# Embedding tower on one core: one store for the codes of all halves, an earlier load of codes and x tile, and an earlier transpose

## The reference

```python
# e: 2048 x 16 x 16, e[:, t] = tbl_t[ids[:, t]]
A = jnp.repeat(r_x0, 16, axis=1)                           # 2048 x 624 x 16
Bm = jnp.repeat(e, 39, axis=2).reshape(2048, 624, 16)
z = jnp.einsum('bnh,bnd,nk,khd,kd->bkh', A, Bm, alpha, w, hv[..., 0])
h = jnp.concatenate([z.reshape(2048, 256), dense_ctx], axis=1)
h = jnp.maximum(h @ W_top1 + b_top1, 0.0)     # 272 -> 512
h = jnp.maximum(h @ W_top2 + b_top2, 0.0)     # 512 -> 256
y = h @ W_top3                                # 256 -> 1
```

## Time and profile before

| | us |
|---|---|
| median of 3 runs | 180.37 |
| the three runs | 180.37, 179.28, 182.56 |
| the profiled execution's own time | 178.92 |
| its span | 177.0 |
| TensorE busy (matmul) | 164.0, 93% |
| VectorE busy | 142.5, 80% |
| GpSimd busy | 110.9, 63% |
| ScalarE busy | 66.0, 37% |

### The profile page before, as it was taken

The page is one execution under the profiler, slowest core; times in us unless marked ns, Lnnn a source line. Parts: engine busy times, 40 slices in busy tenths (PEclk is TensorE's granted clock), DMA queues, the critical chain, the costliest instruction groups (busy, mean ns, idle before and its releaser), DMA issues.

```text
span 177.0 us, 5041 instructions
## 1 busy us (share of the span) xinstructions
PE 164.0 (93%) x2131; PEld 124.3 (70%) x2131; DVE 142.5 (80%) x177; ACT 66.0 (37%) x176; POOL 110.9 (63%) x116
## 2 busy tenths in 40 slices
PE   6549898968997999999999999999999999999993
PEld 1338696736984879696969696969686967776671
DVE  2978797893799999999899979996999899495000
ACT  3440788084881125212431243123403341451141
POOL 2777777777747777777777777777777776000000
PEclk9999999996999999999999999999999999999999
DMA  5889999999999997989498948694559360000000
GB/s 87 307 120 327 246 275 161 270 373 264 283 334 250 345 320 150 363 248 230 79 352 240 216 160 300 189 230 104 183 219 222 48 231 6 2 4 0 0 4 0
DMA packets 15085, 34.26 MB, mean 194 GB/s; under 512 B 6618, under 2 KB 10582, under 8 KB 11990
## 3 DMA queue, kind: packets, MB, share of 16 engines
q1 hardware_dynamic: 10162, 31.51, 58.9%
q0 software_dynamic: 3584, 0.92, 6.6%
q10 hardware_dynamic: 1316, 1.50, 2.9%
HBM read 33.88 MB, written 0.04 MB: 192 GB/s over the span
## 4 chain that ended last, share of the span: by engine, by line
PE 69%; DMA 13%; DVE 4%; ACT 3%; SPq 3%; issue 3%; POOL 3%; DVEq 0%
PE bank L927 17%; PE bank L842 17%; PE bank L848 15%; PE bank L894 11%; DMA ids_half_dram<-ids_half 6%; PE bank L915 5%; PE bank L835 4%; DMA ids_b<-ids_half_dram 3%; POOL e L478 3%; DMA e<-tbl_dram,ids_all 3%; DVE prod L642 2%; SPq L446 2%; DMA ids_all<-ids_dram 1%; ACT apart L724 1%; PE bank L856 1%
## 5 line engine op out<-in xcount | busy, mean ns | idle before, releaser
L478 POOL DMA_INDIRECT e<-tbl_dram,ids_all x112 | 110.7, 988 | 38.7 <-issue 33.2
L642 DVE TENSOR_TENSOR prod<-x,bank 128x2048 f32<-128x2048 f32 x40 | 90.3, 2279 | 8.8 <-issue 4.6
L927 PE MATMUL bank<-prod,m_w 128*32 128x256 f32 x640 | 38.6, 382 | 2.5 <-DVE prod L642 2.5
L894 PE MATMUL bank<-table,onehot 125*128 125x64 bf16 (+1 forms) x288 | 31.9, 198 | 2.3 <-DVE low L537 2.3
L842 PE MATMUL bank<-tower,w_z 128*128 128x256 f32 x128 | 32.8, 403 | 0.7 <-ACT tower L743 0.7
L894 PE MATMUL bank<-low,onehot 125*128 125x64 bf16 (+1 forms) x288 | 31.8, 197 | 0.0
L894 PE MATMUL bank<-rest,onehot 125*128 125x64 bf16 (+1 forms) x288 | 31.8, 199 | 0.0
L894 PEld LDWEIGHTS bank<-table,onehot 125*128 125x128 bf16 x288 | 27.4, 98 | 5.7 <-issue 2.9
L927 PEld LDWEIGHTS bank<-prod,m_w 128*32 128x32 f32 x640 | 19.1, 109 | 17.0 <-issue 3.5
L848 PE MATMUL bank<-tower,w 128*128 128x256 f32 x128 | 30.7, 382 | 0.1
L842 PEld LDWEIGHTS bank<-tower,w_z 128*128 128x128 f32 x128 | 24.2, 199 | 6.3 <-ACT tower L743 3.1
(11 more groups left out here) (60 smaller groups left out, 85.4 us busy)
## 6 DMA issues: line engine op xcount, KB each, us to landing
x<-x_dram SPq DMA_DIRECT2D x16, 1024.0 KB, 8.1
x<-x_dram SPq DMA_DIRECT2D x16, 512.0 KB, 12.4
ids_b<-ids_half_dram SPq DMA_DIRECT2D x7, 576.0 KB
e<-tbl_dram,ids_all POOLq DMA_INDIRECT x112, 4.7
prod<-windows_c_dram ACTq DMA_DIRECT2D x1, 768.0 KB
prod<-windows_c_dram ACTq DMA_DIRECT2D x1, 512.0 KB, 5.6
w_z<-w_z_dram SPq DMA_DIRECT2D x1, 512.0 KB
w<-w_dram SPq DMA_DIRECT2D x1, 512.0 KB, 11.0
```

The source lines that it names most:

```text
L478: nc.gpsimd.indirect_dma_start(out=e[:, tile, f * D:(f + 1) * D], out_offset=None, in_=t[f"tbl_{f}"][:, :], in_offset=bass.IndirectOffsetO ...
L642: nc.vector.tensor_tensor(prod[:, s % NPROD, :].rearrange("p (q b) -> p q b", q=HP), x0[:, tile % NX, :].rearrange("p (q b) -> p q b", q=H ...
L894: made = nc.tensor.matmul(o_bank[i % 2][:, at:at + m * D], onehot[:, n % 2, g, HOT.index(f), tile * P:(tile + 1) * P], parts[part][:, KT_A ...
L927: made = nc.tensor.matmul(z_bank[q * ZW:(q + 1) * ZW, a * HB:(a + 1) * HB], m_w[:, UNIT_OF[g], hp * ZW:(hp + 1) * ZW], prod[:, s % NPROD, ...
```

## The change

All 72 rows of codes go to DRAM by one DMA at the place where half 1's store stood; the six later stores and SyncE's wait for them are gone. On SyncE the load of half 2's codes moves ahead of `b_w3`, and x tile 3 ahead of `ctx` and `w1_z`; x tile 4 moves ahead of half 3's codes and `w2`. On TensorE turn (0, 2) moves ahead of pick 5.

```diff
-        ids_stored = [sem(f"ids_stored_{n}") for n in range(2)]
+        ids_stored = sem("ids_stored")
...
-            sp.dma_start(ids_rows[1], ids_half[1:IDS:NH, :]).then_inc(ids_stored[0], 16)
+            sp.dma_start(ids_rows.rearrange("n f b -> f n b"), ids_half[:]).then_inc(ids_stored, 16)
...
-            sp.wait_ge(ids_stored[0], 16)
+            sp.wait_ge(ids_stored, 16)
             load_ids(1)
             sp.wait_ge(gathered[0][0], 16 * 2 * len(GATHERED[0][0]))
             load_x0(1)
             load_x0(2)
-            for n in range(2, NH):
-                sp.dma_start(ids_rows[n], ids_half[n:IDS:NH, :]).then_inc(ids_stored[1], 16)
+            load_ids(2)
             sp.dma_start(b_w3[:], t["b_w3"]).then_inc(in_b_w3, 16)
+            load_x0(3)
             load_ctx()
             sp.dma_start(w1_z[:], t["w1_z"].rearrange("(a p) n -> p a n", p=P)).then_inc(in_w1, 16)
-            sp.wait_ge(ids_stored[1], 16 * (NH - 2))
-            load_ids(2)
-            load_x0(3)
+            load_x0(4)
             load_ids(3)
             sp.dma_start(w2[:], t["w2"].rearrange("(a p) n -> p a n", p=P)).then_inc(in_w2, 16)
-            load_x0(4)
...
                 if s == 2:
                     for unit in CONTRACTS[2]:
                         contract(unit)
+                    turn_windows(0, 2)
                     for i in PICKS[2]:
                         pick_rows(i)
...
-                if s == 1 or g == 2:
+                if s == 1 or g == 2 and n > 0:
                     turn_windows(n, g)
```

## The result

The changed kernel takes 184.18 us, median of 4 runs (182.02 to 185.93). The kernel before, run beside it, takes 179.82 (4 runs, 179.02 to 182.56). The ratio is 1.0246, 95% interval 1.0176 to 1.0316: about 2.5% slower, where 1.1% faster was forecast, and outside the range. Runs of one kernel scatter by several us here, and the ratios are made from undisturbed runs alone, so a ratio and its two medians needn't agree.

A forecast was written before the change was run, and what follows sets the result against it. TensorE alone sets the end from about 57 us. Step 5 gains 2.5 us, but half 3's codes hold contract 7 to 53.9 instead of 55.87: 2.0 us, so 180.37 becomes 178.4, range 176.4 to 181.5.

The forecast's parts named there:

- The one store: Codes to DRAM: one 36 KB store for seven of 4.5 KB costs 0, with 0 to 1 us allowed.
- Half 2's codes: SyncE's load behind x tile 2: lands by 33.3 to 34.1 us instead of 36.2, so ScalarE leaves the path.
- The turn: TensorE's turn (0, 2) ahead of pick 5: step 3 starts at 33.04, contract 4 ends at 38.6, gain 0.84 us.
- The mark: Contract 7, TensorE's last contraction that has to wait, at 55.87 us; arriving there sooner shortens the run by the same amount.
- `w1_z` lands at 39.2, 0.6 us of waiting: TensorE behind contract 4: the load lands between 38.1 and 40.3 us, middle 39.2, and is wanted at 38.6.
- The base, 33.9: Landing of `w1_z` in the kernel before: 36.2 less the 2.3 us that half 2's codes need at 255 GB/s.
- A second term: Half 3's codes, with x tile 4 now ahead of them: land between 45.1 and 46.3 us, taken as 45.4.
- the prediction's own 8.5 us: ScalarE's path: contract 7 can't start earlier than 8.5 us after `find_apart(3)`, which gave 53.9 us.
- The clock: Rival, chance 0.22: TensorE's clock falls to 1.2 GHz again, l1 loses 1.65 us, gain 0.9, 179.5 us.
- The loads keep pace: Rival, chance 0.15: `w1_z` at 38.1, half 3's codes before 44.2, contract 7 at 52.8, gain 3.0, 177.4 us.
- Half 3's codes come late: Rival, chance 0.13: they land after 47.4 us, contract 7 passes 55.87, slower, say 182.0 us.
- It doesn't do what it says: Rival, chance 0.08: turn (0, 2) waits for a late gather, or the store delays half 1's codes; 180.4 us.

The follow-up runs named there:

- e9: The changed kernel again, unaltered: 183.00 us, ratio 1.0179 to the kernel before.
- e8: The kernel before with the single store for seven, every load in its old order: 180.09 us, ratio 0.9923.
- e15: The changed kernel with `ctx_x` split, the columns of halves 0 and 1 at the old place, the others behind x tile 9: 178.22 us, ratio 0.9936.
- e4: The changed kernel with fourteen products of zeros on TensorE ahead of the wait for `w1_z`: 181.46 us, ratio 1.0157.
- e1: The changed kernel with x tile 3 back behind `w1_z`: 182.84 us, no ratio.
- e6: The changed kernel with x tile 4 back behind `w2`, tile 3 still ahead of `w1_z`: 180.62 us, ratio 0.9984.
- e3: The changed kernel with `w1_z` ahead of the four `ctx` loads: 181.32 us, ratio 1.0007.
- e14: The changed kernel with x tile 3 back behind `w1_z`, x tile 4 back behind `w2`, and `ctx_x` split: 177.13 us, ratio 0.9898.
- e18: The same kernel as e14, measured again: 177.26 us, ratio 0.9919.
- e2: The kernel before with turn (0, 2) ahead of pick 5 and nothing else: 181.30 us, ratio 1.0146.
- e13: The kernel before without the row gathers of halves 1 to 7, their columns set to zero: 179.16 us, no ratio.
- e12: The order of e1 with x tile 4 not loaded at all, its slot zeroed by VectorE: 176.14 us, ratio 0.9922.

## Why the prediction was wrong

| step | forecast | measured |
|---|---|---|
| contract 4 ends | 38.6 | 38.93 |
| `w1_z` lands | 39.2 (38.1 to 40.3) | 41.8; in e9 21.5 us after issue, wait 5.21 |
| waiting for it | 0.6 | 3.15 |
| context part and l1 | 1.13 + 1.89 | 2.07 + 3.78 |
| step 5 | 42.8 | 48.53 |
| half 3's codes land | 45.4 | 47.4 |
| `w2` lands | 47.3 to 48.0 | 49.0 |
| step 5 to contract 7 | 11.1 | 10.57 |
| contract 7 | 53.9 | 59.10 |

**What held.** The one store costs nothing (e8). Half 2's codes came at 30.8, 2.5 us ahead of the forecast, and ScalarE left the path. The turn let steps 3 and 4 follow without a pause, 0.56 us up to contract 4's end (39.49 to 38.93) where 0.84 were forecast. The mark was right: from contract 7 on all shifts along, by 3.2 us at contract 7, at l2 and in the span.

**The step that failed** is the price "`w1_z` lands at 39.2, 0.6 us of waiting". The mechanism was named, its size wrong: it landed at 41.8, and TensorE waited 3.15 us. The trace records a load's landing in up to sixteen pieces, and these show two errors. The base, 33.9, was worked back from half 2's codes as if `w1_z` were all in 2.3 us ahead of them. In the kernel before ten of its sixteen pieces are on record, from 32.2 to 34.9, the last after the first pieces of those codes (34.1). So the base was at least 1.0 us early. From there to 41.8 the moved 1.64 MB cost at most 6.9 us, where I took 5.3, and 6.4 as the most.

They didn't cost it evenly, either. In the changed kernel fourteen of the sixteen pieces were in from 36.5 to 37.8, ahead of the forecast, and the last two came at 40.8 and 41.8. I moved bytes at the mean rate of the queue, 255 to 393 GB/s; TensorE waits for the slowest piece. What holds the last two back no run shows.

The slow `ctx` loads have a part in it, since without 192 KB of them the wait was 1.21 us (e15). But they stand ahead of `w1_z` in the kernel before too, where the same trough lies from 28 to 30 us, 110 and 63 GB/s, and in the changed kernel it is over some 4 us before TensorE begins to wait. So the trough by itself is no term that the forecast left out.

A second term was off and stayed hidden. Half 3's codes, issued at 28.41, landed at 47.4 instead of 45.4:

```profile
28.41 0.51 SPq L415 DMA_DIRECT2D ids_b<-ids_half_dram  x1
28.96 1.32 SPq L452 DMA_DIRECT2D w<-w_dram  x1
```
```profile
ids_b<-ids_half_dram SPq DMA_DIRECT2D x1, 576.0 KB, 19.0
w<-w_dram SPq DMA_DIRECT2D x1, 512.0 KB, 20.0
```

By the prediction's own 8.5 us behind them, contract 7 would have come at 55.9, no earlier than before, even with `w1_z` in time.

**The clock** came with it, as a second cost of the same step. I had it as a rival of its own, with a price of 1.65 us and about 1 us of idle time ahead of it; behind 3.15 us of standing it cost 0.94 + 1.89 = 2.83 us. e4 shows that it goes when TensorE is kept busy. Measured against the forecast, step 5 is 5.73 us late: 0.33 from contract 4, 2.55 more of waiting and 2.83 of clock make 5.71. The Trainium skill (TensorE: Matmul & The Clock Gate, Part 1) has an idle stretch bring the throttle back; the trace agrees, 0.50 behind the wait, 1.00 with products in it.

**The rivals.** "The loads keep pace" was the wrong way round. The Trainium skill (DMA: Bandwidth & Descriptors, Anatomy of one DMA) gives its sum for one DMA that GpSimd issues; these loads are SyncE's, many in one queue. By it I had an estimate of 37.7 for `w1_z`; the trace says 41.8, and the loads ahead moved at 381 GB/s from 28.0 to 31.5 us and at 114 to 116 from 32.5 to 34.5. "Half 3's codes come late" was a true mechanism with the wrong place in the order: the codes came at its very limit, 47.4, but in the changed kernel `find_apart(3)` at 49.09 waits for nothing, because the front is later still; e1 took the first wait away and it waited 5.04 us. "It doesn't do what it says" didn't happen.

**What stays open.** Why the last two pieces of `w1_z` lag. Why tile 4, queued behind `w1_z`, matters (e6), and why e3 and e6 show no loss in their ratios with waits of 2.59 and 3.17 us; so the account of the loss by the wait and the clock is shown for the profiled executions, and for the medians only in part. What the turn is worth by itself: no run shows its 0.84 us, and its sign isn't settled. Whether the 16 partitions, or the short contiguous pieces, make the `ctx` loads slow: no run changed either.

## What to carry to other kernels

Before a load is moved up in a queue, find when the last piece of each load behind it lands, and not only the mean rate of the queue: here fourteen pieces of sixteen were in 4 us ahead of the last. Read the GB/s stretch by stretch: while small loads into few partitions move, the rate can be a third of what it was just before. Price a wait on the tensor engine twice, once for its length and once for the clock behind it. When several waits cover each other, a single edit shows nothing or a loss; look for what is next in line, and try the pair.

## What the runs showed of the hardware

- While the `ctx` loads moved, the DMA engines carried 63 to 116 GB/s in all, at 1.0 to 1.6 of full share; just before, with x tile and codes, it was 381 in the changed kernel. Packets of every load were slow in that stretch. The trace records each DMA packet with its start and duration: in the changed kernel a 1 KB packet took 172 ns (median) from 32.5 to 34.5 us, against 46 from 28.0 to 31.5, and a 2 KB packet of `w1_z` 299 ns, against 96 from 35 to 37.
- One load lands in pieces that can lie far apart: `w1_z` from 36.5 to 41.8 us in the changed kernel, half 3's codes from 44.4 to 47.4.
- TensorE stood at the same instruction in the middle of pick 9 whenever it came there early: 2.48 us in e14, 2.30 in e18, 2.01 in e2, 1.88 in e1, 0.92 in e13, 0.37 in e12, 0.30 in e8. The timeline names no engine or load for it, but the packet records show a 16 KB packet of the queue that the page calls "instruction" just before. In all seven TensorE goes on 1.4 to 1.7 us after that packet ends (in e14 it ends at 47.04 and TensorE goes on at 48.57), and in the other runs it comes to this instruction 1.6 us or more after it. That fits a wait for code; no run changed the code's place to try it.
- The 1.2 GHz level stayed for some time after TensorE was busy again: from 42.1 to 48.0 in the changed kernel it was busy all 5.90 us.
